# Channel-major second MLP matmul and inverse transform, folded first attention normalisation, and spectral mixing by maxima

## The reference

```
part 1   h  = depthwise_conv7x7(x) + conv_b; h = layernorm over channels(h) * g + b
         x1 = x + layer_scale * (gelu(h @ w1 + b1) @ w2 + b2)            # 96 -> 384 -> 96
         u  = relu(batchnorm1(layernorm(x1) @ aw1))                      # 96 -> 192
         X  = fft(u, over the 3136 tokens)
part 2   xr = relu(X.real*rd - X.imag*id + rb); xi = relu(X.imag*rd + X.real*id + ib)
         y  = ifft(xr + i*xi).real
part 3   x2 = x1 + batchnorm2(y @ aw2)                                   # 192 -> 96
         out = x2 + ffn_fp8(layernorm(x2))                               # 96 -> 384 -> 96, products in float8
```

## Time and profile before

| | |
|---|---|
| median of 3 runs | 4698.79 us (4695.02 to 4704.4) |
| the profiled execution: its own time | 4703.32 us |
| its span, first to last instruction | 4701.3 us, mean TensorE clock 0.955 |
| PE busy | 4316.8 us, 92% |
| DVE busy | 3481.5 us, 74% |
| ACT busy | 2557.6 us, 54% |
| POOL busy | 1408.7 us, 30% |

### The profile page before, as it was taken

One profiled execution on the slowest core, in us unless ns is written; L12 is line 12 of the kernel. 1 busy time (PEld: TensorE's weight loads), 2 busy tenths in 40 slices (PEclk: granted clock), 3 DMA queues, 4 the chain that ended last, 5 costly groups with the idle time before them and its releaser, 6 DMA issues.

```text
span 4701.3 us, 100572 instructions
## 1 busy us (share of the span) xinstructions
PE 4316.8 (92%) x28624; PEld 3532.8 (75%) x28624; DVE 3481.5 (74%) x13109; ACT 2557.6 (54%) x5282; POOL 1408.7 (30%) x1060
## 2 busy tenths in 40 slices
PE   4999969999999999999999999999999999999986
PEld 2444438888888888888888888888888888888874
DVE  1333335788888888888888888888888888888877
ACT  2343325565565655555556655555565565565653
POOL 1111153333333333333333333333333233333321
PEclk7999979999999999999999999999999999999996
DMA  5666623444444444444333434344444444444331
GB/s 137 170 170 170 170 85 91 109 111 116 113 113 111 116 111 116 113 111 115 100 100 105 110 103 108 105 112 111 114 111 115 113 115 111 113 115 111 105 90 51
DMA packets 427312, 536.67 MB, mean 114 GB/s; under 512 B 219591, under 2 KB 385131, under 8 KB 411051
## 3 DMA queue, kind: packets, MB, share of 16 engines
q1 hardware_dynamic: 412558, 510.37, 40.2%
q10 hardware_dynamic: 14272, 20.04, 1.7%
HBM read 295.17 MB, written 235.12 MB: 113 GB/s over the span
## 4 chain that ended last, share of the span: by engine, by line
PE 78%; issue 4%; DVE 2%; DMA 1%; ACT 1%; POOL 0%; SPq 0%; POOLq 0%; DVEq 0%; ACTq 0%
PE psum L974 12%; PE psum L987 11%; PE psum L984 8%; PE psum L1030 7%; PE psum L1021 7%; PE psum L1010 6%; PE psum L1002 6%; PE psum L1044 4%; PE psum L1037 3%; PE psum L1066 3%; PE psum L1059 3%; PE psum L994 2%; PE psum L967 2%; PE psum L1051 2%; PE psum L1070 2%
## 5 line engine op out<-in xcount | busy, mean ns | idle before, releaser
L683 POOL TENSOR_TENSOR sums<-sums,minus_half 112x4 f32<-112x4 f32 (+1 forms) x480 | 631.0, 1318 | 2127.4 <-DVE sums L829 2127.4
L703 POOL TENSOR_SCALAR minus<-minus 96x448 f32<-96x448 f32 (+1 forms) x512 | 640.9, 1252 | 640.9 <-DVE minus L868 619.0
L974 PE MATMUL psum<-hn,w_sb 96*128 96x448 f32 x1344 | 613.4, 597 | 162.0 <-issue 160.2
L987 PE MATMUL psum<-w_sb,hid 128*112 128x96 f32 x5376 | 679.6, 263 | 0.0
L987 PEld LDWEIGHTS psum<-w_sb,hid 128*112 128x112 f32 x5376 | 617.6, 181 | 0.0
L744 ACT ACTIVATE hid<-psum,b_sb 128x448 f32<-128x448 f32 x672 | 418.1, 637 | 336.9 <-PE psum L974 298.6
L974 PEld LDWEIGHTS psum<-hn,w_sb 96*128 96x128 f32 x1344 | 262.8, 208 | 364.4 <-issue 354.0
L386 PE MATMUL c_psum<-c_xt,c_toeplitz 128*112 128x448 f32 x1152 | 479.3, 554 | 48.9 <-ACT c_xt L328 23.1
L834 DVE TENSOR_SCALAR xn<-t,sums 112x96 f32<-112x96 f32 x1792 | 514.4, 349 | 7.4 <-POOL sums L683 7.4
L414 DVE TENSOR_SCALAR c_h<-c_psum,c_bias 112x448 f32<-112x448 f32 x192 | 199.0, 1037 | 430.1 <-PE c_psum L386 430.1
L984 PE MATMUL psum<-skip,x_sb 97*112 97x96 f32 x1792 | 503.7, 363 | 2.4 <-ACT hid L744 2.4
(11 more groups left out here) (82 smaller groups left out, 7471.4 us busy)
## 6 DMA issues: line engine op xcount, KB each, us to landing
outer_spectrum<-outer SPq DMA_DIRECT2D x448, 168.0 KB
inner<-outer_spectrum SPq DMA_DIRECT2D x32, 2016.0 KB
c_xpad<-x SPq DMA_DIRECT2D x96, 392.0 KB, 11.2
h_tokens<-c_h SPq DMA_DIRECT2D x24, 1568.0 KB, 8.3
h<-h_tokens SPq DMA_DIRECT2D x32, 1176.0 KB, 13.2
x_sb<-x SPq DMA_DIRECT2D x32, 1176.0 KB, 8.0
residual_stream<-t SPq DMA_DIRECT2D x224, 168.0 KB, 2.1
inner_inverse<-unmixed SPq DMA_DIRECT2D x224, 168.0 KB, 2.4
```

Of the source, the lines that this page charges most:

```text
L683: nc.gpsimd.tensor_tensor(su[:, :, 6], su[:, :, 5], minus_half[:, 0:su.shape[1]], ALU.pow).then_inc(ready.sem, 1)
L703: nc.gpsimd.tensor_scalar(part, part, 0.0, None, ALU.max).then_inc(clipped.sem, 1)
L974: pe.matmul(bank("M1", c, m, CW, 128), w1_sb[:, m * 128:(m + 1) * 128], hn[:, c * CW:(c + 1) * CW], start=True, stop=True).then_inc(m1_mad ...
L987: last = pe.matmul(dst[:, j * C:(j + 1) * C], hid[:, c % 2, m, j * PT:(j + 1) * PT], w2_sb[:, m, :], start=False, stop=(m == KF - 1))
```

## The change

M2 and the outer inverse AP become channel-major: 96 channels on the partitions, 448 tokens along them.

- **M2**: three matmuls of 448 columns with w2 as weights. DVE adds b2 and the residual x from `x_sb`, read with a step of 28 elements, and writes t1. PE transposes t1 (T) for the statistics alone, which DVE reads in PSUM.
- **N is gone.** W1 multiplies the not normalised t1 by weights that subtract the mean over the channels. DVE instead of ACT writes act1 as max(product * deviation, -shift), and a 113th row puts the shift back in A.
- **B and C**: relu(a) + relu(b) is written with maxima; ACT's `uw` has another sign for its second half, DVE's `plus` and `minus` take a maximum instead of a sum, and POOL forms `both` from them in two instructions per half of the channels. DVE's C and POOL's clip are gone.
- **AP**: 112 columns per matmul instead of 96. A new step S2 transposes t2 (PE), copies it to `t2_rows` (ACT) and takes the statistics from there (DVE). The transposes of t2 in F2 are gone, and the result adds t2 from SBUF.
- The statistics take five small instructions instead of six, and rings, places and a few prepared constants change.

```diff
+    2: {"B": (11, 9.3, ND), "W": (24, 9.3, ND), "IB": (28, 8.8, ND)},
+    3: {"AP": (3, 11.5, NC), "S2": (8, 11.5, NC), "N2": (14, 11.5, NC), "T2": (18, 11.5, NC), "F1": (20.5, 12, NC),
...
+JOBS = {"HT": [("act", 1)], "M1": [("act", 3)], "B": [("spec", 2)], "M2": [("dve", 1)], "W": [("act", 1)],
+        "IB": [("act", 1)], "T": [("dve", 1)], "W1": [("dve", 2)], "A": [("act", 2)], "AP": [("dve", 1)],
+        "S2": [("act", 1)], "T2": [("act", 1)], "F1": [("act", 3)], "F2": [("act", 1)]}
+RING = {"act": 4, "dve": 2, "spec": 2}
...
-                            part = minus[:, j % 2, :, 0:chunk_pairs(c) * PT // 2]
-                            nc.gpsimd.tensor_scalar(part, part, 0.0, None, ALU.max).then_inc(clipped.sem, 1)
+                            for k in range(2):
+                                def half(t):
+                                    return t[:, j % 2, k, 0:w * PT // 2].rearrange("p (s k) -> p s k", s=w)
+                                last = nc.gpsimd.tensor_tensor(
+                                    both[:, c % 2, m, 0:w, k * PT // 2:(k + 1) * PT // 2], half(plus), half(minus),
+                                    ALU.subtract if k else ALU.add)
+                            last.then_inc(both_done.sem, 1)
...
+                    if name == "S2":
+                        act.wait_ge(rows2_made.sem, rows2_made.at(n, c))
+
+                        act.wait_ge(xn2_done.sem, xn2_done.at(*before(n, c, NC, 2)))
+                        nc.scalar.copy(t2_rows[:, c % 2, :, :].rearrange("p t c -> p (t c)"),
+                                       bank("S2", c, 0, CH * C, PT)).then_inc(rows2_done.sem, 1)
...
+                        dve.wait_ge(m2_made.sem, m2_made.at(n, c))
+
+                        b, j = before(n, c, NC, 4)
+                        dve.wait_ge(t1_stored[c % 4].sem, t1_stored[c % 4].at(b, j // 4))
+                        dve.wait_ge(a1_made.sem, a1_made.at(b, 2 * j + 1))
+                        dve.wait_ge(rows1_made.sem, rows1_made.at(b, j))
+                        nc.vector.scalar_tensor_tensor(
+                            out=t1[:, c % 4, :].rearrange("c (q p) -> c q p", q=CH),
+                            in0=bank("M2", c, 0, CW, C).rearrange("c (q p) -> c q p", q=CH), scalar=b2_sb[:, 0:1],
+                            in1=x_sb[:, :].rearrange("c (p q) -> c q p", q=NQ)[:, part, :], op0=ALU.add, op1=ALU.add
+                            ).then_inc(t1_done.sem, 1)
+                    if name == "T":
+                        dve.wait_ge(rows1_made.sem, rows1_made.at(n, c))
+                        see(1, bank("T", c, 0, CH * C, PT).rearrange("p (t c) -> p t c", t=CH), 0
+                            ).then_inc(ln_step[1].sem, 1)
+
+                        dve.wait_ge(ln1_ready.sem, ln1_ready.at(*before(n, c, NC, 1)))
                         variances(1, n, c, LN_EPS, ln1_seen)
...
+                        for m in range(2):
+                            j = 2 * c + m
+                            dve.wait_ge(a1_made.sem, a1_made.at(n, j))
+
+                            dve.wait_ge(outer_made.sem, outer_made.at(*before(n, j, 2 * NC, 4)))
+                            z = bank("W1", c, m, 2 * H2, PT)
+                            for k in range(2):
+                                at = CH * (c % 2) + 2 * m + k
+                                last = nc.vector.scalar_tensor_tensor(
+                                    out=act1[0:PT, j % 4, k, :], in0=z[:, k * H2:(k + 1) * H2],
+                                    scalar=scales[1][:, at:at + 1], in1=below[:, :], op0=ALU.mult, op1=ALU.max)
+                            last.then_inc(act1_done.sem, 1)
...
-                                        in0=im, scalar=spec[:, m, at:at + 1], in1=u, op0=ALU.mult, op1=ALU.add)
+                                        in0=im, scalar=spec[:, m, at:at + 1], in1=u, op0=ALU.mult, op1=ALU.max)
...
+                        dve.wait_ge(rows2_made.sem, rows2_made.at(b, j))
+                        dve.wait_ge(result_done.sem, result_done.at(b, j))
+                        nc.vector.tensor_tensor(t2[:, c % 4, :], bank("AP", c, 0, CW, C), t1_old[:, c % 3, :], ALU.add
                                                 ).then_inc(t2_done.sem, 1)
-                        dve.wait_ge(t2_done.sem, t2_done.at(n, c))
-                        see(2, dst, 0).then_inc(ln_step[2].sem, 1)
+                    if name == "S2":
+                        dve.wait_ge(rows2_done.sem, rows2_done.at(n, c))
+                        see(2, t2_rows[:, c % 2, :, :], 0).then_inc(ln_step[2].sem, 1)
+
+                        b, j = before(n, c, NC, 1)
+                        dve.wait_ge(ln2_ready.sem, ln2_ready.at(b, j))
+                        dve.wait_ge(xn2_done.sem, xn2_done.at(b, j))
...
-                        dst = bank("M2", c, 0, CH * C, PT)
+                        dst = bank("M2", c, 0, CW, C, "dve")
                         pe.wait_ge(gelu_done.sem, gelu_done.at(n, KF * c + KF - 1))
-                        for j in range(CH):
-                            q = CH * c + j
-
-                            pe.matmul(dst[:, j * C:(j + 1) * C], x_sb[:, q:q + (PT - 1) * NQ + 1:NQ], skip[:, :],
-                                      start=True, stop=False)
-                            for m in range(KF):
-                                last = pe.matmul(dst[:, j * C:(j + 1) * C], hid[:, c % 2, m, j * PT:(j + 1) * PT],
-                                                 w2_sb[:, m, :], start=False, stop=(m == KF - 1))
+                        for m in range(KF):
+                            last = pe.matmul(dst, w2_sb[:, m, :], hid[:, c % 2, m, :], start=(m == 0), stop=(m == KF - 1))
...
+                        dst = bank("T", c, 0, CH * C, PT, "dve")
+                        pe.wait_ge(t1_done.sem, t1_done.at(n, c))
...
-                        dst = bank("AP", c, 0, CH * C, PT, "dve")
+                        dst = bank("AP", c, 0, CW, C, "dve")
                         for j in range(CH):
-                            last = pe.matmul(dst[:, j * C:(j + 1) * C], outer_inv[:, CH * c + j, :],
-                                             back[:, CH * c + j, :], start=True, stop=True)
+                            last = pe.matmul(dst[:, j * PT:(j + 1) * PT], back[:, CH * c + j, :],
+                                             outer_inv[:, CH * c + j, :], start=True, stop=True)
                         last.then_inc(o_made.sem, 1)
+                    if name == "S2":
+                        dst = bank("S2", c, 0, CH * C, PT)
+                        pe.wait_ge(t2_done.sem, t2_done.at(n, c))
+                        for j in range(CH):
+                            last = pe.transpose(dst[:, j * C:(j + 1) * C], t2[:, c % 4, j * PT:(j + 1) * PT], ident[0:C, 0:C])
+                        last.then_inc(rows2_made.sem, 1)
...
-                        dst = bank("F2", c, 0, CW, C, "dve")
-                        for j in range(CH):
-                            last = pe.transpose(dst[:, j * PT:(j + 1) * PT], t2[:, c % 4, j, :], ident[0:PT, 0:PT])
-                        last.then_inc(t2t_made.sem, 1)
```

More of the change, by code:

```diff
@@ L582, in turns @@
             turn("end", NB + 1)
-        constant_rows(nc, wts, x_sb, xnt, inner, back)
+        constant_rows(nc, wts, inner, back, act1, psum)
         credit_all(nc, signals)
@@ L1091, in _ @@
         def _(dve):
[L1092 to L1093 removed]
+            nc.vector.memset(constant, 0.0).then_inc(rows_set, 1)
+            dve.wait_ge(rows_set, 1)
+            nc.vector.memset(constant.rearrange("o (q m) -> o q m", m=2 * K1)[:, :, 0:1], PT / NTOK ** 0.5).then_inc(rows_set, 1)
+            dve.wait_ge(centred, 1)
+            nc.vector.tensor_copy(wts.aw1[:, :], psum[0:C, 0, 0:H2])
+        @block.tensor
+        def _(pe):
+            pe.matmul(psum[0:C, 0, 0:H2], wts.centre[:, :], wts.aw1[:, :], start=True, stop=True).then_inc(centred, 1)
 def hn_tiles(hn, c):
@@ L1182, in weight_loads @@
     ]
-    loads += [(raw.bn1[:, k, :], spread(bn1[k], C + 1, H2)) for k in range(4)]
+    loads += [(raw.bn1[:, k, :], spread(bn1[k], PT, H2)) for k in range(4)]
     loads += [(raw.bn2[:, k, :], spread(bn2[k], C, C)) for k in range(4)]
```

222 lines of the change are left out of this document (95 added, 127 removed).

## The result

The changed kernel takes 4679.07 us (median of 6 runs, 4678.01 to 4682.92), the kernel before 4697.97 us beside it. The ratio is 0.9963, 95% interval 0.9952 to 0.9974: faster by 0.4%. The forecast was 4846 us, slower by 3%.

The account below looks back on a forecast made before the run. Past 20 us into a turn PE and DVE were taken as level. DVE -1.1 and waits +6.5 made +5.4 us a turn, +162 in all; with -20 and +5, 4850 profiled, 4846 for runs, range 4550 to 4930.

Parts of the forecast that it names:

- The waits that come: At a turn's start PE and DVE wait for each other around T2: +8.1 us, +6.5 after filling short gaps.
- the sum: Whole run: +5.4 us a turn, +162 over 30 turns, with -20 and +5 elsewhere, giving 4850 profiled, 4846 us for runs.
- PE -11.8 us a turn: M2 on PE falls from 3.96 to 2.28 us a chunk, seven chunks a turn; other PE changes come to 0.
- DVE's load -1.1: DVE's work a turn: 16.5 us removed, 15.4 added, so -1.1 us, bounds -3.1 and +2.4.
- M2's add: DVE's new add of M2, reading x_sb with a step of 28: 0.82 us each, 5.7 a turn, bounds 4.5 and 6.9.
- GpSimd beside DVE, put at 0: POOL's paired adds replace its clip; their contention with DVE changes nothing: 0, bounds -2 and +4 us a turn.
- The turns before the loop -20: The "first" and "second" turns have PE full and DVE not, so PE's saving counts: 20 us less for both.
- constants +5: Constants of the second phase take ten small DMAs more: 5 us.
- The twice slower case: Rival: PE's new idle places lower its clock and POOL's adds double, +5 us a turn more, 4996 us; chance 0.13.
- Nothing changes: Rival: gains and waits cancel within 0.2% (9 us); chance 0.05.
- Faster, the chain at the start does not bind: Rival: N2's result is there when PE reaches T2/0 and T2/1; a turn 2.8 to 4.8 us shorter, 4564 us; chance 0.27.
- The forecast's own range: Whole run: 4740 to 4950 us, from DVE's bounds (-3.1, +2.4) and the waits (5 to 8.1).

Follow-up runs that it names:

- e3: Changed kernel with one semaphore increment that nothing waits for ahead of each step of PE's loop turn, about 1631 instructions: 4679.37 us.
- e11: Changed kernel with two semaphore increments that nothing waits for ahead of each step of PE's loop turn, about 1767 instructions: 4992.47 us (one run).
- e2: Changed kernel with three semaphore increments that nothing waits for ahead of each step of PE's loop turn, about 1903 instructions: 5095.48 us.
- e6: Kernel before with the 29 turns of its loop written out, so without the jump: 4504.64 us.
- e1: Kernel before with only M2's matmuls on PE replaced by three of 448 columns, residual and right columns left out: 4363.36 us.
- e8: Changed kernel, DVE's add of M2 reading x_sb without the step of 28, so other tokens' values are added: 4725.57 us.
- e4: Changed kernel with the second normalisation (N2) put 2.5 places earlier in DVE's list: 4732.78 us.
- e9: Changed kernel with the second normalisation (N2) put 0.6 places earlier in DVE's list, ahead of B/0 and G: 4767.75 us.
- e12: Changed kernel with T's statistics (0.9 instead of 2 later) and the second normalisation (0.6 earlier) both ahead of DVE's first maxima: 4721.36 us.
- e13: Changed kernel with three PSUM banks each for DVE's and ACT's rings, instead of two and four: 4780.16 us.
- e15: Changed kernel with T2 transposing the rows before normalisation, so PE does not wait for DVE there; the MLP gets other values: 4713.71 us.
- e16: Changed kernel with S2 one place earlier in PE's list, ahead of M2 in chunks 1 to 3: 4747.65 us.

## Why the prediction was wrong

- **The failed step: "The waits that come" and, with it, the sum took the jump as unchanged.** M1/0 was placed with the 4.84 us of the earlier trace rows, and a turn's 10.6 us wait for AP, named as the loop's jump, "in which nothing runs", was left in both kernels. In its place the runs showed a jump whose cost hangs on the length of PE's loop body: nothing up to about 1631 instructions, nine refetched packets a turn from 1767 on (e3, e11, e2), and 194 us for the kernel before (e6). The page of the profile had its sign, 282 packets on the instruction queue. The change takes PE's body from the one side to the other, and no term stood for that. With the body on the far side again the changed kernel takes 4992 us (e11, with its increments): for a jump that stays as it was, the forecast had the right direction.
- **PE -11.8 us a turn, off the bound: right.** From start to start M2 takes 2.3 us at full clock (2063.69 to 2066.02) for 3.96. PE's busy share by the forecast's own numbers would be 105.1 of 128.7 us, 82% and not 83%. What it is worth with DVE left alone is e1 beside e6: another 141 us.
- **DVE's load -1.1: nearly.** Measured 102.2 to 101.6. The mis-sized term is M2's add: 0.97 us from start to start (2066.51 to 2067.48) for 0.82, so 1.05 us a turn more; it was within its bounds. e8 shows the step of 28 as the reason, 1030 against 676 ns. W1's 0.33 each, GpSimd's adds (668 ns, forecast 0.7) and the statistics came as worked out. The 0.97 us lie between the two estimates that the forecast worked out from the Trainium skill, "Vector Engine (DVE) Microarchitecture Reference", section 5.2, 0.8 us for long jumps and 1.1 for small steps.
- **The waits, +6.5: right in place and nearly in size.** T2/0 waits 4.27 us (3.2 forecast), T2/1 2.61 (2), S2/1 3.36 (1.9), S2/2 3.23 (3.3), B/0 1.82 (2.1), `act` 2.1 (2.6). The turn written out went from 116.6 to 123.7 us, +7.1 where +5.4 was forecast, and the whole by 202 us where the sum had 147.
- **GpSimd beside DVE, put at 0: a term that moved.** Of the 1.07 us by which T2/0 waits longer than forecast 0.86 are N2/0 itself. It takes 1.81 us from start to start (2073.67 to 2075.48) for 0.95, with two of GpSimd's adds beside it, and N2/1 without them takes 0.95 (2092.73 to 2093.68):

```profile
2073.93 1.33 POOL L712 TENSOR_TENSOR both<-plus,minus 96x224 f32<-96x224 f32 x2 [0.17 <-DVE minus L892]
...
2092.73 1.04 DVE L831 TENSOR_SCALAR xn<-t_rows,sums,scales 112x96 f32<-112x96 f32 x4
```

Before, N/0 stood in that place and PE did not wait for it. (The forecast's "0.93 us took 1.71" sets a start-to-start time beside a busy time; from start to start that one took 1.35.)
- **The turns before the loop -20, constants +5: in part.** From the first load to the loop -7.9 us, and -13.6 ahead of it, where the forecast had no gain; that part is open.
- **After the result the waits were read too literally.** The theory of e4 and e9 took them as links of a chain, so that an earlier link gains. Seven edits that moved or removed a link or took load off DVE (e4, e8, e9, e12, e13, e15, e16) all ended above the changed kernel, by 35 to 101 us, with clocks of 0.93 to 0.96. How much of that is the clock and how much DVE's lag they do not separate.
- **The rivals.** The twice slower case named the clock behind new idle places; it is real (M2/1 3.75 us) but costs 1.3 us a turn here, because it falls at one place only. Nearest in time came "Nothing changes": the result is 20 us under 4699, outside its 9 us, and gains and waits did nearly cancel, but by a gain that it did not name. "Faster, the chain at the start does not bind" lies at 4564 us, and its condition fails, as T2/0 and T2/1 wait. That 4679 us lie within the stated range (4550 to 4930) is luck: the range was widened for that rival, and two effects of some 200 us of opposite sign met, one of which stood nowhere. The forecast's own range, 4740 to 4950, misses it.

What stays open: which part of the change makes the turn longer by these 7 us (the normalisation folded into W1, M2's sum on DVE, or the maxima with GpSimd's sums). e1 leaves all three out, and no run took them one by one. That the clock falls behind a gap was seen in e8, e9, e12 and e15; what decides whether it does was not found.

The fastest kernel with the reference's result among these is e6, the kernel before with its turns written out: 4504.64 us, 3.7% under the changed one.

## What to carry to other kernels

Before a change that adds or removes many instructions of a looping engine, look at the instruction queue's packets and at the "issue" wait behind the jump: they tell whether the body is fetched anew each turn, and so whether some hundred instructions fewer, or the loop written out, may by themselves be worth what they were here, 7 us a turn. Where two engines are level and wait for each other, a wait in the trace tells where the lag is noticed and not what it is worth; take the wait away with everything else left as it is (as e15) before the order is tuned by it. And watch TensorE's clock in each such trial, since 2.5 us less of DVE's work a turn went with a loss here (e8).
